# Graph attention on one core: ScalarE scales the running sums, VectorE adds the bias and the bases, and the row sums come earlier

## What is computed

```python
xn = _layernorm(x, axis=-1)
x = x + _L0_gnn_ref(xn, edge_index, ...) + _L0_mix_ref(xn[None], ...)[0]
x = x + _L0_ffn_ref(_layernorm(x, axis=-1)[None], ...)[0]
```

```python
msg = xl[src] + xr[dst]
act = jnp.where(msg > 0, msg, NEG_SLOPE * msg)
e = jnp.einsum('ehd,hd->eh', act, att)
p = jnp.exp(e - m[dst])
out = jax.ops.segment_sum(alpha[..., None] * xl[src], dst, num_segments=n)
```

## Time and profile before

| | |
|---|---|
| median of 3 runs | 975.21 us (972.39 to 977.58) |
| profiled execution, its own time | 969.87 us |
| span of the profiled execution | 968.1 us |
| mean granted clock of TensorE | 0.959 |
| busy, share of the span: PE | 861.4 us, 89% |
| PE weight load | 418.8 us, 43% |
| DVE | 841.0 us, 87% |
| ScalarE (ACT) | 555.2 us, 57% |
| GpSimd (POOL) | 508.8 us, 53% |

### The profile page before, as it was taken

The page is one execution under the profiler, slowest core; times in us unless marked ns, Lnnn a source line. Parts: engine busy times, 40 slices in busy tenths (PEclk is TensorE's granted clock), DMA queues, the critical chain, the costliest instruction groups (busy, mean ns, idle before and its releaser), DMA issues.

```text
span 968.1 us, 9537 instructions
## 1 busy us (share of the span) xinstructions
PE 861.4 (89%) x2734; PEld 418.8 (43%) x2734; DVE 841.0 (87%) x971; ACT 555.2 (57%) x1949; POOL 508.8 (53%) x529
## 2 busy tenths in 40 slices
PE   4979999999949999999999899991999988989754
PEld 3865455644415444443443344440444443434321
DVE  7999989769999999999988899799886059999995
ACT  3303124237676887878879797887778042443332
POOL 5200363557667777677777677687786620010001
PEclk9989999999988999999999999996999999999968
DMA  9231724443543433554335533339721211123124
GB/s 295 89 126 13 215 56 159 137 164 89 85 163 117 150 91 94 176 179 116 95 101 171 175 95 101 87 89 232 291 71 40 71 43 44 48 61 61 27 43 82
DMA packets 64946, 109.97 MB, mean 114 GB/s; under 512 B 29223, under 2 KB 36036, under 8 KB 64874
## 3 DMA queue, kind: packets, MB, share of 16 engines
q0 software_dynamic: 19856, 55.42, 22.6%
q1 hardware_dynamic: 45034, 53.92, 17.0%
HBM read 89.15 MB, written 17.17 MB: 110 GB/s over the span
## 4 chain that ended last, share of the span: by engine, by line
DVE 53%; issue 15%; PE 13%; ACT 13%; DMA 3%; POOL 1%; another core or an unknown queue 1%; SPq 0%; DVEq 0%; POOLq 0%; ACTq 0%
PE acc L759 10%; ACT round_mem L1116 10%; DVE acc_sb L1486 7%; DVE z L1634 6%; DVE turned L1632 6%; DVE turned L1478 4%; DVE round_mem L1232 3%; DVE round_mem L1236 2%; DVE round_mem L1231 2%; DVE round_mem L1228 2%; DVE round_mem L1233 2%; ACT pz L1103 2%; DVE round_mem L1229 2%; DVE round_mem L1230 2%; DVE big_b L1440 1%
## 5 line engine op out<-in xcount | busy, mean ns | idle before, releaser
L559 POOL DMA_INDIRECT round_mem<-msg_table,idx x352 | 344.2, 978 | 134.2 <-issue 80.5
L1116 ACT ACTIVATE round_mem<-round_mem,pz 128x65 f32<-128x65 f32 x1408 | 358.0, 398 | 32.4 <-issue 14.0
L759 PE MATMUL acc<-wslot,big_a 128*128 128x512 f32 x512 | 225.4, 601 | 7.8 <-ACT big_b L1049 3.8
L759 PEld LDWEIGHTS acc<-wslot,big_a 128*128 128x128 f32 x512 | 97.8, 193 | 133.8 <-issue 123.9
L1486 DVE TENSOR_REDUCE acc_sb<-round_mem 128x260 f32<-128x1820 f32 (+1 forms) x62 | 121.6, 1962 | 33.7 <-ACT round_mem L1116 19.0
L759 PE MATMUL acc<-big_b,wslot 128*128 128x512 f32 x256 | 112.1, 600 | 5.1 <-remote 3.5
L1103 ACT ACTIVATE pz<-z 128x7 f32<-128x7 f32 (+1 forms) x248 | 56.5, 296 | 103.0 <-DVE z L1639 77.2
L759 PE MATMUL acc<-wslot,big_b 128*128 128x512 f32 x256 | 110.0, 592 | 0.0
L1478 DVE TENSOR_TENSOR turned<-round_mem,turned 128x1560 f32<-128x1560 f32 (+1 forms) x62 | 105.4, 1700 | 2.7 <-DMA round_mem<-msg_table,idx 0.4
L1634 DVE TENSOR_REDUCE z<-turned 128x24 f32<-128x1560 f32 (+1 forms) x62 | 105.1, 1695 | 2.1
L1632 DVE SCALAR_TENSOR_TENSOR turned<-turned,att_sb 128x1536 f32<-128x1536 f32 (+1 forms) x62 | 103.5, 1670 | 0.0
(11 more groups left out here) (222 smaller groups left out, 1060.2 us busy)
## 6 DMA issues: line engine op xcount, KB each, us to landing
big_b<-in_x SPq DMA_DIRECT2D x18, 512.0 KB, 6.0
round_mem<-msg_table,idx POOLq DMA_INDIRECT x352
out_x<-big_b SPq DMA_DIRECT2D x9, 512.0 KB, 2.7
out_x<-acc_sb POOLq DMA_DIRECT2D x9, 512.0 KB, 5.3
wslot<-in_wv_t SPq DMA_DIRECT2D x2, 2048.0 KB
wslot<-in_wk_t SPq DMA_DIRECT2D x2, 2048.0 KB
wslot<-in_wo_t SPq DMA_DIRECT2D x2, 2048.0 KB
wslot<-in_wq SPq DMA_DIRECT2D x2, 2048.0 KB
```

What stands on the lines that cost most here:

```text
L559: pool.indirect_dma_start(xg[g % 4][:, j, :], None, msg_table, bass.IndirectOffsetOnAxis(idx[:, c, j0 + j:j0 + j + 1], 0)).then_inc(xg_in[ ...
L759: mm = nc.tensor.matmul(o(acc[:, n % 4, :]), a, b, start=first, stop=last)
L1116: ins = nc.scalar.activation(to[:, :, j], xg[g % 4][:, j, h * HR + 1:(h + 1) * HR], ACT.Copy, scale=pz[:, g % 2, j, h:h + 1])
```

## The change

1. `rescale` leaves GpSimd. ScalarE scales the running sums with four instructions of 65 columns, one a head, behind the weighted rows of the same round. The semaphore `rescaled` and DVE's wait for it go.
2. `add_bias` and `add_base` leave GpSimd for DVE: the bias for chunks 0 to 7 in the rounds 54 to 61, one each, the rest behind the rounds.
3. The first eight `sum_p0` stand before round 0, the other eight in rounds 0 to 3. `sum_bias` stands in the rounds 41 to 48.
4. PE's small product for the offsets (line 795) stands behind the last two `hid` groups, not before them.
5. SP loads `bv` and `bk` before the store of the last piece of weights and the 2 MB load of view 4.
6. `PRODUCTS_AT` is 173, not 179: most banks are due one round earlier.

```diff
-PRODUCTS_AT, GROUP_STEP = 179.0, {"p0c": 2.0, "bias": 1.0}
+PRODUCTS_AT, GROUP_STEP = 173.0, {"p0c": 2.0, "bias": 1.0}
+BIAS_SUMS_AT, X_AT = 41, 54
...
-            for q in range(8, 12):
+            for q in range(8, 11):
                 store(q)
-            sp.wait_ge(w_quantized, 3)
-            sp.dma_start(view(4), uses[4][1]).then_inc(w_in[0], 16)
             sp.wait_ge(acc_full, index_of["gram", 15] + 1)
             sp.dma_start(bv_bc, bv.rearrange("(a d) -> a d", a=1).to_broadcast([P, D])).then_inc(vb_in, 16)
             sp.dma_start(bk_bc, bk.rearrange("(a d) -> a d", a=1).to_broadcast([P, D])).then_inc(vb_in, 16)
+            store(11)
+            sp.wait_ge(w_quantized, 3)
+            sp.dma_start(view(4), uses[4][1]).then_inc(w_in[0], 16)
...
                 for j in range(n):
-                    if j == 4 and g >= 3:
-                        rescale(g - 3)
...
-                if g > LAST - 6:
-                    add_bias(g - (LAST - 5))
-            for g in range(LAST - 2, LAST + 1):
-                rescale(g)
-                add_bias(6 + g - (LAST - 2))
...
-            for c in range(EARLY):
-                add_base(c)
-            add_bias(C - 1)
...
-                if n == 4:
-                    pe.wait_ge(tot_done, 1)
-                    pe.wait_ge(pool_const, 10)
-                    nc.tensor.matmul(tp[0:DG_HI, 1, 0:1], tri, tot[:], start=True, stop=True).then_inc(off_done, 1)
...
+            pe.wait_ge(xt_taken, 2 * C)
+            pe.wait_ge(tot_done, 1)
+            pe.wait_ge(pool_const, 10)
+            nc.tensor.matmul(tp[0:DG_HI, 1, 0:1], tri, tot[:], start=True, stop=True).then_inc(off_done, 1)
...
                     for j in range(slots):
-                        ins = nc.scalar.activation(to[:, :, j], xg[g % 4][:, j, h * HR + 1:(h + 1) * HR], ACT.Copy, scale=pz[:, g % 2, j, h:h + 1])
+                        nc.scalar.activation(to[:, :, j], xg[g % 4][:, j, h * HR + 1:(h + 1) * HR], ACT.Copy, scale=pz[:, g % 2, j, h:h + 1])
+                for h in range(H):
+                    to = halves_of[g % 3][:, h // 2, (h % 2) * MR:(h % 2 + 1) * MR, :]
+                    ins = nc.scalar.activation(to[:, :, slots], running[c][:, h * MR:(h + 1) * MR], ACT.Copy, scale=pz[:, g % 2, slots, h:h + 1])
                 ins.then_inc(mul_done, 1)
...
                 dve.wait_ge(mul_done, g + 1)
-                dve.wait_ge(rescaled, g + 1)
...
+            def add_bias(c):
+
+                n = rows(c)
+                dve.wait_ge(x_in[c], 32)
+                ins = nc.vector.tensor_tensor(base[0:n, c, :], x_last if c == C - 1 else base[:, c, :], bias_bc[0:n, :], ALU.add)
+                ins.then_inc(bias_added, 1)
+
+            def add_base(c):
+
+                dve.wait_ge(acc_taken["act"], taken[index_of["base", ORDER["base"].index((c, 1))]])
+                b = base[:, c, :].rearrange("p (k n) -> p k n", k=KB)
+                step(nc.vector.tensor_tensor(b, base_at[c], b, ALU.add))
...
+            for n in range(KB):
+                sum_p0(n)
...
-                if 1 <= g <= 8:
-                    sum_p0(2 * g - 2)
-                    sum_p0(2 * g - 1)
-                if 46 <= g < 46 + KB:
-                    sum_bias(g - 46)
+                if g < KB // 2:
+                    sum_p0(KB + 2 * g)
+                    sum_p0(KB + 2 * g + 1)
+                if BIAS_SUMS_AT <= g < BIAS_SUMS_AT + KB:
+                    sum_bias(g - BIAS_SUMS_AT)
+                if X_AT <= g < X_AT + C - 2:
+                    add_bias(g - X_AT)
             close(LAST)
             for n in due("dve", None):
                 take(n)
+            add_bias(C - 2)
+            dve.wait_ge(bias_added, C - 1)
+            for c in range(EARLY - 1):
+                add_base(c)
+            add_bias(C - 1)
+            dve.wait_ge(bias_added, C)
+            add_base(EARLY - 1)
```

More of the change, by code:

```diff
@@ L267, in gps_layer @@
         colsum_done, colsum2_done = sem("colsum_done"), sem("colsum2_done")
-        rescaled = sem("rescaled")
         p0_summed, bias_summed = sem("p0_summed"), sem("bias_summed")
@@ L274, in gps_layer @@
         act_step = sem("act_step")
-        base_added, bias_added = sem("base_added"), sem("bias_added")
+        bias_added = sem("bias_added")
         x2_full, x2_taken = sem("x2_full"), sem("x2_taken")
@@ L529, in _ @@
             sp.wait_ge(added[1], 16 * 4)
-        round_of, freed, at = {}, {}, PRODUCTS_AT
-        for n in range(index_of["p", 0], len(groups)):
-            kind, i, _ = groups[n]
-            at = max(at, freed.get(n - 4, 0))
-            at += GROUP_STEP.get(kind, 7.0)
-            round_of[n] = max(0, math.ceil((at - ROUND_0_AT) / ROUND_STEP))
-            if kind == "base" and ORDER["base"][i][1] == 1:
-                round_of[index_of["base", ORDER["base"].index((ORDER["base"][i][0], 0))]] = round_of[n]
-            freed[n] = max(at, ROUND_0_AT + round_of[n] * ROUND_STEP) + 1.5
         @block.gpsimd
@@ L986, in _ @@
                     x2(*i)
+        round_of, freed, at = {}, {}, PRODUCTS_AT
+        for n in range(index_of["p", 0], len(groups)):
+            kind, i, _ = groups[n]
+            at = max(at, freed.get(n - 4, 0))
+            at += GROUP_STEP.get(kind, 7.0)
+            round_of[n] = max(0, math.ceil((at - ROUND_0_AT) / ROUND_STEP))
+            if kind == "base" and ORDER["base"][i][1] == 1:
+                round_of[index_of["base", ORDER["base"].index((ORDER["base"][i][0], 0))]] = round_of[n]
+            freed[n] = max(at, ROUND_0_AT + round_of[n] * ROUND_STEP) + 1.5
         def due(engine, g):
@@ L1582, in residual @@
             def residual(c, h):
-                dve.wait_ge(base_added, min(c + 1, EARLY))
-                if c == C - 1:
-                    dve.wait_ge(bias_added, C)
                 dve.wait_ge(x2_full, x2_made.index((c, h)) + 1)
@@ L1611, in sum_p0 @@
                 ins.then_inc(p0_summed, 1)
+            def add_bias(c):
[7 more added lines that the diff above has]
+                step(nc.vector.tensor_tensor(b, base_at[c], b, ALU.add))
+            assert round_of[index_of["bias", 1]] < X_AT <= LAST - (C - 3)
             def sum_bias(k):
```

27 lines of the change are left out of this document (removed).

## The result

| | before | after |
|---|---|---|
| median | 974.67 us (972.39 to 977.58, 4 runs) | 967.56 us (965.38 to 968.06, 4 runs) |
| ratio to before, 95% interval | | 0.9917 (0.9892 to 0.9943) |
| profiled execution, its own time | 969.87 us | 965.38 us |
| span | 968.1 us | 963.5 us |
| ScalarE busy | 555.2 us | 614.7 us |

The change makes the kernel 0.8% faster. The prediction was 1002 us, slower. A second set of runs gave a ratio of 0.9903 (0.9878 to 0.9928).

A forecast was written before the change was run, and what follows sets the result against it. The prediction took a ScalarE fed at a limited pace to set the rounds: +39.9 for their end, -12.8 behind them, +27.1 on 969.9 gives 997.0, plus 5.3 for the median: 1002 us. Range 980 to 1030, 8 in 10 within 952 to 1030.

The forecast's parts named there:

- +39.9: End of the edge-attention rounds: ScalarE's last product 39.9 us later, at 788.6 us instead of 748.7.
- -12.8: Between the rounds and the first residual: distance shrinks from 31.3 to 18.5 us, giving back 12.8 us.
- ScalarE's pace: Rounds: ScalarE fed at a limited pace, 3.22 per us read at 440 to 612 us; 1946 instructions take 580 us.
- PE is then ahead of the rounds, not on the path: 0: PE's small product moved and sums earlier: PE's waits go, but this gains 0.
- What stands between the rounds and the tail: After the rounds: a take, the last pair of base groups, a take and first product up to the residual, 18.5 us.
- Sums ahead of round 0: Before round 0: eight sums fill DVE's gap, round 0 starts unchanged, 6.8 us of sums leave the next rounds.
- Rescaling: Rounds: ScalarE gains 248 products, unhindered 0.96 us a round; its round is longer than DVE's from round 26 on.
- Additions on DVE: Rounds 54 to 61 and after: 9.6 us of bias additions hidden if ScalarE is behind, about 9 us beside PE.
- Rival A: Rounds: ScalarE is not held, holes do not grow, base groups become the limit; 950 us median, chance 0.28.
- Rival B: Rounds: holes as large as now, no larger; -4.7 us, 970 us median; chance 0.15 with the even zone.
- What would show it: Signs: ScalarE 3.3 to 3.4 per us, holes before 390 us, DVE waiting over 33.7, rounds near 9.4, residual 18 us behind.
- The two PE waits: PE: waits of 12.4 us for the p0 sums and 20.0 us for the bias sums both go.

The follow-up runs named there:

- e3: Kernel before, with ScalarE writing four more products a round into a spare array nobody reads, GpSimd keeping the rescaling: ratio 1.0026.
- m2: No computation, ScalarE's products alone, beside loads, beside gathers, on a chip that pauses: full pace in the first two, 214 products in 205 us beside gathers.
- m3: No computation, ScalarE's products beside gathers, with GpSimd adding nothing, 260 or 1024 columns after every six: 72, 72 and 419 products in 100 us.
- e2: Kernel before with only the rescaling moved from GpSimd to ScalarE: ratio 1.0015.
- e6: Kernel before with only the bias sums moved five rounds earlier, to rounds 41 to 48: ratio 1.0027.
- e9: Kernel before with the bias sums in rounds 41 to 48 and the table of banks from 173, not 179: ratio 0.9915.
- e1: Changed kernel with only the rescaling put back on GpSimd: 953.6 us, ratio 0.9825 to the kernel before.
- e5: Changed kernel with the rescaling and the bias and base additions all back on GpSimd: ratio 0.9805 to the kernel before.
- e4: Changed kernel with the bias and base additions back on GpSimd: 959.1 us, ratio 0.9877 to the kernel before.
- e12: Changed kernel with a new bank table (products from 176, round 0 at 200, rounds of 8.4 us): ratio 0.9762 to the kernel before.
- m1: No computation, ScalarE's products alone, beside loads, beside gathers, on the chip without pauses: 4.2 products per us whatever runs beside it.

## Why the prediction was wrong

- **In the terms of the sum**: "+39.9" for the end of the rounds was +1.5, "-12.8" for the distance from there to the first residual was -8.1 (23.2 us against 31.3), and the tail, put at nothing, was +1.9. Together, before rounding, -4.6 us, where +27.1 was forecast.
- **ScalarE's pace** ("3.22 per us", "580 us"): wrong, and the largest term. The stretch 440 to 612 us showed no limit. ScalarE was busy 144 of its 172 us; of the 28 us of idle time the profile gives 18.6 to issue, 6.5 to an unknown origin and 0.7 to `z`. With 74 more instructions the same stretch has 12.4 us of idle time and 3.65 per us, and e3, which leaves GpSimd as it was, does 641 there, 3.73 per us. So most of that idle time was room that more products could fill. The rounds took 543.3 us and ended 1.5 us later, not 39.9. The kind of mechanism was right (on m2's chip ScalarE can be held at a limited pace), but m2 and m3 reach its limit only while GpSimd's gathers follow each other closely, and I put a rate measured at one load on another load. e2 and e3, at 0 to 0.3% for 248 products on the kernel before, are the direct test.
- **"PE is then ahead of the rounds, not on the path: 0"**: wrong, and this is where the gain is. PE's last 14 groups ended 27.5 us behind the rounds. Its wait of 20.0 us for the bias sums stood before them. What I should have asked is what else holds the base groups once that wait goes: the take of the last `t2` bank, at 678.9 us in round 54, one round earlier by the new table. e6 and e9 show both halves. I used that take for the base groups' start myself, but only in a sum in which the rounds were 82 us long from there, so that PE had time.
- **What stands between the rounds and the tail** (18.5 us): 23.2. The rounds from the take on lasted 79.5 us (670.7 to 750.2), not 82 plus a pair, and PE needed 98.5. Of these some 2 are the clock: after the 13.6 us of idle time TensorE was granted 0.50 to 0.63 until 676 us (0.50 is 1.2 GHz), and the first group took 9.0 us from its start to that of the next, the others 6.87. With the tail's start at 773.4 the forecast misses by 33.7 us: 788.6 + 18.5 = 807.1. The windows of after around that idle time:

```profile
658.00:671.00 13.00, 0.00 (x0) 0.00 (x0) 11.13 (x13) 12.88 (x53) 7.95 (x9) 0.65 1.21 208
671.30:674.00 2.70, 2.70 (x3) 1.17 (x4) 2.60 (x4) 2.22 (x10) 1.95 (x3) 0.50 1.17 206
674.00:676.00 2.00, 2.00 (x4) 0.87 (x3) 2.00 (x2) 2.00 (x10) 1.54 (x2) 0.63 1.18 280
676.00:678.00 2.00, 2.00 (x6) 0.95 (x5) 1.97 (x2) 1.64 (x7) 1.39 (x3) 1.00 1.20 236
```

- **Sums ahead of round 0**: nearly right in place, 6.8 us foretold for the rounds behind. The first `z` came 1.5 us earlier, and round 10 had it at 295.07 us instead of 304.56, 9.5 us. I gave this no weight because the slow ScalarE was to swallow it. It does so partly: by round 30 only 1.5 us are left (e1 keeps 8.8 there).
- **Rescaling**: 0.96 us a round was right as a price on ScalarE, and "from round 26 on it is the longer one" was late: it is so in many rounds from 12 on. What reaches the end is 9 us (e1 against after by ratio), not 40, and next to nothing on the kernel before (e2). The rule of the Trainium skill that I weighed against it (ScalarE: Activation LUTs, Rules for kernel authors) points the right way: e1 without the edit is faster. That VectorE would be the better place was not tried; GpSimd was.
- **Additions on DVE**: hidden, as foretold, within 0.3% (e5 against e1, e4 against after).
- **Rival A** was right that nothing grows by much, and had the structure that decided (base groups as the limit after the rounds), but priced them from shorter rounds. It asked for 3.74 instructions per us, and e12 shows, on the chip without pauses, 1948 in rounds of 517.7 us, 3.76. **Rival B** came nearest, 970 against 967.6, for the wrong reason: the pauses did not stay as large as they were (39 to 66), the gain came past them. **What would show it**: pauses before 390 us and DVE's wait over 33.7 us came true, the round length (8.8, not 9.4) and the 18 us did not. The two PE waits went, and I had not named the one that took their place.
- The page cited for rival A (Runtime: NRT & Kernel Launch, Instruction fetch mechanics, of the Trainium skill) says that fetching is hidden behind the pace of issue. No run shows that the pauses are fetches. If they are, m1 agrees with the page, and m2 and m3 do not: while GpSimd sent gathers an instruction came in every 1.40 us on those chips. The trace of m2 speaks against slow packets as the cause. Its page has 23 packets in 0.19 MB on the queue for instructions, 8 KB each. While ScalarE goes at full pace one comes every 30.7 us, and each takes 0.3 to 0.6 us. In the slow stretch, 455 to 686 us, there are three, at 474.9, 556.1 and 662.8 us, of 0.31 to 0.40 us, and the products between them still come singly every 1.40 us. Where the instructions are held behind these packets, or whether it is the instructions at all, stays open.

## What to carry to other kernels

When two chains share the engines, follow each to where they meet and ask of both what holds them there; a wait that is "off the path" on one chain may be the path of the other. When a wait goes, look up what releases the same engine next: an edit that is worth nothing alone (e6) may be worth something with a second one (e9). A rate read where an engine has idle room is no limit of that engine; a table that places takes in rounds has to be made with the rounds' real length.

## What was not expected of the hardware

On two chips ScalarE's instructions came in at one per 1.40 us while GpSimd sent gathers back to back (m2 and m3: 72 in 100 us, where a third chip did 419 with m1). On one of them, in m3, 0.63 us of other work after every six gathers did not help, and 1.9 us brought the full pace back. After back-to-back gathers ScalarE stayed slow for 27 us more. On the third chip, m1's, the kernel before is 2% faster (953.4 us against 971.6 to 974.2), and the kernels traced there show one to three pauses instead of 39 to 66. What in the chips makes the difference is open, and wider instructions of ScalarE or other engines beside gathers were not tried. TensorE, idle for 13.6 us, ran its next 5 us at a granted clock of 0.50 to 0.63.
